# Scan stage of a two-layer decoder: C read through DMA-repeated rows, both readings on GpSimd, operand splits divided over three places

## What is computed

```python
xp = jnp.einsum('bld,ed->ble', x, Wx)          # 64 + 2 * 16 columns
dt_x, B, C = xp[..., :64], xp[..., 64:80], xp[..., 80:96]
dt = softplus(einsum('blr,dr->bld', dt_x, Wdt) + bdt)
dA  = exp(einsum('bld,dn->bldn', dt, A))       # n = 16 states
dBx = einsum('bld,bln,bld->bldn', dt, B, x)
h_t = dA_t * h_{t-1} + dBx_t
y_t = einsum('bdn,bn->bd', h_t, C_t);  y = y + x * D
```

## Time and profile before

| | us |
|---|---|
| median of 3 runs | 1063.38 (1063.21 to 1065.33) |
| profiled execution | 1063.77 |
| its span | 1061.7 |
| busy in the span: PE, DVE, ACT, POOL | 910.1, 805.7, 685.1, 519.6 |
| mean granted TensorE clock | 0.949 of 2.4 GHz |
| scan loop, first product to last reading | 264.7 to 395.9 |
| cross attention, g = 0 to 31 | from about 425 |

### The profile page before, as it was taken

How to read it: one execution, slowest core, us unless ns; L and a number is a source line. 1 busy time by engine, 2 the same in 40 slices (tenths; PEclk the granted TensorE clock), 3 DMA queues, 4 the chain that set the end, 5 groups by cost and what they waited for, 6 DMA issues and landing times.

```text
span 1061.7 us, 16111 instructions
## 1 busy us (share of the span) xinstructions
PE 910.1 (86%) x5404; PEld 578.2 (54%) x5420; DVE 805.7 (76%) x1360; ACT 685.1 (65%) x1601; POOL 519.6 (49%) x407
## 2 busy tenths in 40 slices
PE   5888899565667675799999999999999898999998
PEld 3666544242222222566666777777777565656665
DVE  4578789898999998778888777777877766654554
ACT  2656479787899834788777776887776355532232
POOL 4322346351787832667777666667665443400000
PEclk9899899887798998999999999999999999999999
DMA  9832104000000000000000062111002421222221
GB/s 331 328 137 101 59 18 161 9 1 0 0 1 0 1 0 0 1 1 2 1 1 22 23 174 81 40 41 38 1 1 68 149 64 51 71 66 90 68 65 43
DMA packets 36390, 61.32 MB, mean 58 GB/s; under 512 B 5106, under 2 KB 25010, under 8 KB 34772
## 3 DMA queue, kind: packets, MB, share of 16 engines
q1 hardware_dynamic: 36308, 60.30, 17.3%
HBM read 59.17 MB, written 1.12 MB: 57 GB/s over the span
## 4 chain that ended last, share of the span: by engine, by line
PE 46%; DVE 24%; issue 11%; ACT 11%; POOL 5%; DMA 2%; SPq 0%; DVEq 0%; ACTq 0%; POOLq 0%
PE ps L2414 12%; PE ps L2443 6%; ACT ps L2254 5%; DVE arena L1118 4%; PE ps L1978 3%; DVE ps L1114 3%; PE ps L1991 3%; PE ps L451 2%; PE ps L1970 2%; DVE arena L1123 2%; POOL arena L2335 2%; PE ps L1945 1%; PE ps L491 1%; DMA wide<-in_w_down 1%; PE ps L727 1%
## 5 line engine op out<-in xcount | busy, mean ns | idle before, releaser
L2335 POOL TENSOR_TENSOR arena<-arena 128x4 f32<-128x4 f32 x96 | 98.8, 1029 | 44.6 <-DVE arena L2100 41.9
L2246 ACT ACTIVATE arena<-ps,ones 128x512 f32<-128x512 f32 x96 | 68.2, 786 | 60.5 <-PE ps L1952 60.5
L2461 DVE TENSOR_TENSOR arena<-ps,arena 128x512 f32<-128x512 f32 (+1 forms) x56 | 38.7, 691 | 90.2 <-ACT ps L2454 90.2
L2254 ACT ACTIVATE ps<-ps,arena 128x128 f32<-128x128 f32 x256 | 89.3, 365 | 21.5 <-DVE arena L2079 21.5
L2454 ACT ACTIVATE ps<-ps,arena 128x512 f32<-128x512 f32 (+1 forms) x56 | 36.9, 660 | 87.9 <-PE ps L2414 87.6
L2414 PE MATMUL ps<-XT,wide 128*128 128x512 f16 (+1 forms) x384 | 92.3, 379 | 1.1 <-DVE arena L2480 0.9
L2079 DVE TENSOR_REDUCE arena<-ps 128x4 f32<-128x512 f32 x64 | 43.7, 689 | 53.3 <-PE ps L1962 53.3
L2443 PE MATMUL ps<-wide,arena 128*128 128x256 f16 (+1 forms) x672 | 83.0, 274 | 0.1
L1945 PE MATMUL ps<-wide,arena 128*128 128x512 f16 x256 | 66.8, 396 | 13.7 <-ACT arena L2246 7.1
L2443 PEld LDWEIGHTS ps<-wide,arena 128*128 128x128 f16 (+3 forms) x672 | 65.8, 98 | 20.6 <-issue 1.8
L1118 DVE TENSOR_TENSOR_SCAN arena<-arena,ps 128x1024 f32<-128x1024 f32 x32 | 73.2, 2287 | 1.5 <-POOL arena L1257 0.5
(11 more groups left out here) (343 smaller groups left out, 2426.4 us busy)
## 6 DMA issues: line engine op xcount, KB each, us to landing
arena<-comb_rows SPq DMA_DIRECT2D x26, 256.0 KB, 3.1
side<-in_wproj SPq DMA_DIRECT2D x4, 1024.0 KB, 5.4
arena<-in_w_down SPq DMA_DIRECT2D x7, 512.0 KB, 3.9
wide<-in_w_down SPq DMA_DIRECT2D x1, 3584.0 KB, 16.3
side<-in_w_gate SPq DMA_DIRECT2D x1, 3520.0 KB, 18.8
side<-in_w_up SPq DMA_DIRECT2D x1, 3520.0 KB, 12.0
wide<-in_w_gate SPq DMA_DIRECT2D x2, 1728.0 KB, 12.0
side<-in_w_up SPq DMA_DIRECT2D x3, 1024.0 KB, 9.2
```

The source lines that it names most:

```text
L2246: act.activation(flat(turned[g % 2][:, MAXB * j:MAXB * j + MAXB, :]), ps[:, j, :], ACT.Identity, scale=wt[:, 0:1], bias=wt[:, 1:2]).then_i ...
L2254: last = act.activation(ps[:, 4 + t, i * P:(i + 1) * P], ps[:, 4 + t, i * P:(i + 1) * P], ACT.Exp, bias=mx[:, t, i:i + 1], accum_out=den[: ...
L2335: pool.tensor_tensor(rs[:, j, :], var[:, j, :], minus_half[:, j, :], ALU.pow).then_inc(rs_ready, 1)
```

## The change

B stays as it was: PE spreads its row for each step, now always into banks 2c of PSUM. C is written to DRAM once (`rows_dram`, 16 rows of 1024) from `dt_rows`, into which ACT now copies all 96 rows instead of 64; SP then brings row n back repeated over the 128 partitions, into one of two buffers `c_rows`, once the readings of n - 2 are done. `c_copy`, its ACT copy and C's spreading go. POOL makes both readings. DVE has only products and scans in the loop. ACT and POOL have one split in each n (16 in the loop), five more behind the loop (`TAIL`, buffers unsplit[0] and c_rows[0]; they stand ahead of the cross attention's stream on both engines), and one each in iterations 2, 4, 6, 8 and 10 of the cross attention (`later`, one buffer). The chunks are put into another order, so that the first 21 are what the first iterations need; PE waits for 21 before the first projection and for all 26 in iteration 15. SP's small loads for the cross attention move ahead of the rows.

```diff
...
     dA = [A.take([N]) for _ in range(2)]
-    c_copy = A.take([N])
+    c_rows = [A.take([N])]
     state = [A.take([N]) for _ in range(2)]
...
     unsplit = [A.take([k.proj.SPLIT]), k.XN[:, 0:k.proj.SPLIT // D, :].rearrange("p b d -> p (b d)")]
+    c_rows.append(A.take([N]))
+    assert A.at <= 15080, A.at
+    rows_dram = k.nc.dram_tensor("scan_rows", (NST, N), F32, kind="Internal").ap()
     A = Arena(k.arena, 15080)
...
-    dt_rows = state[1]
+    dt_rows = c_rows[1]
     R0, R1 = DTR, DTR + 2 * NST
...
     b_psum = k.sem("sc_b_psum")
-    c_psum = k.sem("sc_c_psum")
+    c_moved = [k.sem(f"sc_c_moved{i}") for i in range(2)]
     dA_ready = k.sem("sc_dA_ready")
...
     state_ready = k.sem("sc_state_ready")
-    c_taken = k.sem("sc_c_taken")
     read0_ready = k.sem("sc_read0_ready")
...
     def banks(i):
         return ps[:, i:i + 2, :].rearrange("p a b -> p (a b)")
-
-    def home(n, c):
-
-        return 2 * ((n + c) % 2)
...
     def sync(sp):
...
             sp.dma_start(dst, src).then_inc(w_loaded, 16)
+        k.load_cross_small(sp)
+        sp.wait_ge(low_ready, 2)
+        sp.dma_start(rows_dram, dt_rows[R0 + NST:R1, :]).then_inc(c_moved[1], 16)
+        sp.wait_ge(c_moved[1], 16)
+        for n in range(NST):
+            if n == 1:
+                sp.wait_ge(dt_psum, 2)
+                sp.wait_ge(parts_ready, 1)
+            wait(sp, read1_ready, n - 1)
+            sp.dma_start(c_rows[n % 2], rows_dram[n:n + 1, :].broadcast_to([P, N])).then_inc(c_moved[n % 2], 16)
...
     def vector(dve, link):
...
-        dve.wait_ge(low_psum, 2)
-        rows = banks(6)[R0:R1, :]
+        dve.wait_ge(low_ready, 2)
+        rows = dt_rows[R0:R1, :]
         link(dve.tensor_copy(high, rows))
...
         for i, (n, c) in enumerate(STEPS):
-            product = banks(home(n, c))
+            product = banks(2 * c)
             dve.wait_ge(b_psum, i + 1)
...
             dve.tensor_tensor_scan(state[c], dA[c], product, 0.0, ALU.mult, ALU.add).then_inc(state_ready, 1)
-            if c:
-                dve.wait_ge(state_ready, i + 1)
-                dve.wait_ge(c_taken, n + 1)
-                wait(dve, summed, 2 * n - 1)
-                dve.tensor_tensor(read[1], state[1], banks(home(n, 0)), ALU.mult).then_inc(read1_ready, 1)
...
         dve.wait_ge(k.xt_psum, 12)
-        dve.wait_ge(w.split, len(w.chunks))
+        dve.wait_ge(w.split, NST)
         dve.wait_ge(summed, len(STEPS) - 1)
...
             act.wait_ge(low_psum, j + 1)
-            act.copy(dt_rows[0:DTR, 512 * j:512 * j + 512], ps[0:DTR, 6 + j, :]).then_inc(low_ready, 1)
+            act.copy(dt_rows[0:R1, 512 * j:512 * j + 512], ps[0:R1, 6 + j, :]).then_inc(low_ready, 1)
         for c in range(KC):
...
                            scale=decay[:, c, n:n + 1]).then_inc(dA_ready, 1)
-            if i < len(w.chunks):
-                w.split_scalar(act, i, unsplit[i % 2])
-            if c:
-                act.wait_ge(c_psum, n + 1)
-                wait(act, read0_ready, n)
-                act.copy(c_copy, banks(home(n, 0))).then_inc(c_taken, 1)
+            if c == 0:
+                w.split_scalar(act, n, unsplit[n % 2])
+        for i in range(NST, NST + w.TAIL):
+            if i == NST + 1:
+                act.wait_ge(read1_ready, NST - 1)
+            w.split_scalar(act, i, (unsplit[0], c_rows[0])[i % 2])
...
     def tensor(pe):
...
-        def spread(n, first, bank, done):
+        def spread(n, c):
...
             for j in range(2):
-                last = pe.matmul(ps[:, bank + j, :], pick[0:K3, first + n:first + n + 1].broadcast_to([K3, P]), parts[0:K3, 512 * j:512 * j + 512],
+                last = pe.matmul(ps[:, 2 * c + j, :], pick[0:K3, n:n + 1].broadcast_to([K3, P]), parts[0:K3, 512 * j:512 * j + 512],
                                  start=True, stop=True)
-            last.then_inc(done, 1)
+            last.then_inc(b_psum, 1)
...
         def accumulate(i):
...
         pe.wait_ge(parts_ready, 1)
-        spread(0, 0, home(0, 0), b_psum)
+        spread(0, 0)
         pe.wait_ge(dt_relu, 2)
-        spread(0, 0, home(0, 1), b_psum)
+        spread(0, 1)
         for n in range(NST):
-            if n:
-                accumulate(2 * n - 1)
-            pe.wait_ge(state_ready, 2 * n + 1)
-            spread(n, NST, home(n, 0), c_psum)
             if n:
...
             if n + 1 < NST:
+                pe.wait_ge(state_ready, 2 * n + 1)
+                spread(n + 1, 0)
+            if n:
+                accumulate(2 * n - 1)
+            if n + 1 < NST:
                 pe.wait_ge(state_ready, 2 * n + 2)
-                spread(n + 1, 0, home(n + 1, 0), b_psum)
-                pe.wait_ge(read1_ready, n + 1)
-                pe.wait_ge(c_taken, n + 1)
-                spread(n + 1, 0, home(n + 1, 1), b_psum)
+                spread(n + 1, 1)
         accumulate(len(STEPS) - 2)
...
         for i, (n, c) in enumerate(STEPS):
-            if i < len(w.chunks):
-                w.split_pool(pool, i, unsplit[i % 2])
-            if c == 0:
-                pool.wait_ge(c_taken, n + 1)
-                pool.wait_ge(state_ready, i + 1)
-                wait(pool, summed, 2 * n)
-                pool.tensor_tensor(read[0], state[0], c_copy, ALU.mult).then_inc(read0_ready, 1)
+            if c:
+                w.split_pool(pool, n, unsplit[n % 2])
+            else:
+                pool.wait_ge(c_moved[n % 2], 16 * (n // 2 + n % 2 + 1))
+            pool.wait_ge(state_ready, i + 1)
+            wait(pool, summed, i - 1)
+            pool.tensor_tensor(read[c], state[c], c_rows[n % 2], ALU.mult).then_inc((read0_ready, read1_ready)[c], 1)
+        for i in range(NST, NST + w.TAIL):
+            w.split_pool(pool, i, (unsplit[0], c_rows[0])[i % 2])
...
         self.centring += [self.kvx[:, c, 0:G * HD] for c in range(KC)]
-        self.chunks = [(k.wide, self.base[m] + c * self.COLS[m] + n, self.factor[:, c, j:j + 1])
-                       for j, m in enumerate(self.ORDER) for c in range(KC)
-                       for n in range(0, self.COLS[m], self.SPLIT)]
+        def of(*names):
+            return [(k.wide, self.base[m] + c * self.COLS[m] + n, self.factor[:, c, j:j + 1])
+                    for j, m in enumerate(self.ORDER) if m in names for c in range(KC)
+                    for n in range(0, self.COLS[m], self.SPLIT)]
+
+        half = NQ * D
+        self.chunks = of("q", "k", "v")
+        self.chunks += [(k.side, n, self.ranged[:, 6:7]) for n in range(0, half, self.SPLIT)]
+        self.FIRST = len(self.chunks)
+        self.chunks += [(self.ct, n, self.ranged[:, 5:6]) for n in range(0, KC * B * S, self.SPLIT)]
         self.chunks += [(k.wide, n, self.ranged[:, 4:5])
                         for n in range(self.kvx_at, self.kvx_at + KC * 2 * G * HD, self.SPLIT)]
-        self.chunks += [(self.ct, n, self.ranged[:, 5:6]) for n in range(0, KC * B * S, self.SPLIT)]
-        self.chunks += [(k.side, n, self.ranged[:, 6:7]) for n in range(0, 2 * NQ * D, self.SPLIT)]
+        self.chunks += of("qx")
+        self.chunks += [(k.side, half + n, self.ranged[:, 6:7]) for n in range(0, half, self.SPLIT)]
...
     def raw(self, m, c):
...
-    def split_scalar(self, act, i, tmp):
+    TAIL = 5
+
+    def split_scalar(self, act, i, tmp, buffers=2):
         if i == 0:
...
         tensor, at, scale = self.chunks[i]
-        wait(act, self.split, i - 1)
+        wait(act, self.split, i + 1 - buffers)
         act.mul(tmp, tensor[:, at:at + self.SPLIT], scale).then_inc(self.scaled, 1)
...
         self.combT = a.take([4 * S])
+        self.weights_at = a.at
         self.weights = [a.take([4 * S]) for _ in range(3)]
...
     beside = range(19, 19 + moe.EARLY)
+    later = range(2, 2 + 2 * (len(w.chunks) - NST - w.TAIL), 2)
+    unsplit = k.arena[:, moe.weights_at:moe.weights_at + w.SPLIT]
     squaring = (12, 14, 18, 19, 20, 21, 22)
...
     def place(g):
...
-    def sync(sp):
-        sp.wait_ge(k.x_done, 2)
+    def load_small(sp):
         for dst, src in ((norms, a["head_norms"]), (smooth, a["smooth"]),
...
         moe.load_small(sp, w_loaded)
+
+    k.load_cross_small = load_small
+
+    def sync(sp):
         sp.wait_ge(xq_ready, B)
...
         turn_x(0)
-        pe.wait_ge(w.split, len(w.chunks))
+        pe.wait_ge(w.split, NST + w.TAIL)
         for j in range(3):
...
             nxt = g + 1 < NG
+            if g + 1 == 2 * B:
+                pe.wait_ge(w.split, len(w.chunks))
             if nxt:
...
                     take_turned(g + 1, j)
+            if g in later:
+                w.split_scalar(act, NST + w.TAIL + later.index(g), unsplit, 1)
             if g in squaring:
...
                 round_c(g - 1)
+            if g in later:
+                w.split_pool(pool, NST + w.TAIL + later.index(g), unsplit)
             if g % 2 == 0 and 0 < g and (g + 4) // 2 < B:
...
```

## The result

| | before | after |
|---|---|---|
| median | 1063.21 (5 runs, 1061.60 to 1065.33) | 1070.36 (5 runs, 1067.89 to 1072.03) |
| profiled execution, and its span | 1063.77, 1061.7 | 1067.89, 1066.1 |
| busy in the span: PE, DVE, ACT, POOL | 910.1, 805.7, 685.1, 519.6 | 894.8, 778.6, 671.5, 557.9 |

A forecast was written before the change was run, and what follows sets the result against it. VectorE was taken to bound the scan loop (8.16 us per n), a ring of engine waits the cross attention's first half. -13.6 + 9.05 = -4.55 from 1063.77 gave 1059.2, less 0.39 for the median 1058.8; range 1054.5 to 1064.5.

The forecast's parts named there:

- Each split costs 1.81, five of them 9.05 us lost: Cross attention, iterations 2, 4, 6, 8, 10: ScalarE's part delays 1.36 us, GpSimd's late roots a further 0.45.
- pairs of 27.01 for 27.0: Cross attention, g from 2 to 11: two iterations were to take 27.0 us instead of 25.2.
- the square root 14.0 earlier for 13.6: Behind the scan loop: batch 0's square root was to move from 402.69 to 389.1, 13.6 us saved.
- The loop: Scan loop: VectorE stays the bound at 3.46 us per step, 6.92 per n, with GpSimd over 95% busy.
- The rows of C: Scan loop: row DMAs land in 4 to 5 us, below the 6.9 available, so they cost nothing.
- the rival of late rows: Scan loop: rows landing at 8 us lose 7.7 us, giving 1066.5; chance 0.07.
- The end of the loop: Behind the loop: table load stands directly behind the last cast, no longer hidden; square root at 389.1, 13.6 us saved.
- What the five splits give back there was put at 6: Behind the loop: the splits delay the square root from about 383 to 389.1, giving back 6 of some 20 us.
- VectorE held by the splits: Cross attention: each GpSimd split holds a bf16 tensor_scalar 1.64 us, five cost 8.2, giving 1067.0; chance 0.13.
- The loop does not get it: Scan loop: GpSimd's waits raise the period to 7.18 us, 4.2 lost, giving 1063.0, no change; chance 0.08.
- The splits cost less: Cross attention: only ScalarE's part costs, 6.8 us, giving 1056.5, or all hidden, 1049.8; chance 0.12.
- the rival that came nearest: Cross attention: VectorE's bf16 tensor_scalar held by the splits, 8.2 us lost, giving 1067.0; chance 0.13.

The follow-up runs named there:

- Experiment 1: Changed kernel with GpSimd's split behind add_x instead of in front of it in cross-attention iterations 2, 4, 6, 8, 10: 1057.94 us, 0.9925 of before.
- Experiment 6: Changed kernel with all 26 splits in the scan loop, none behind it or in the cross attention: 1064.67 us, 1.0004 of before.
- experiment 10: Experiment 9 with three splits behind the loop, seven late ones in iterations 11 to 17, and add_x(2) at the head of iteration 1: 1042.67 us, 0.9796 of before.
- experiment 2: Changed kernel with ten splits behind the loop (TAIL = 10) and none in the cross attention: 1060.61 us, 0.9963 of before.
- experiment 3: Changed kernel with ScalarE's scale and cast ahead of the three turned tiles and GpSimd's split behind add_x: 1059.90 us, 0.9953 of before.
- experiment 4: Experiment 3, but with GpSimd's split ahead of add_x as in the changed kernel: 1059.71 us, 0.9940 of before.
- experiment 9: Changed kernel, late splits in iterations 11 to 15, cast ahead of turned tiles, GpSimd's part behind round_c, TensorE's wait divided: 1051.34 us, 0.9882 of before.

## Why the prediction was wrong

The forecast of 1058.8 was wrong, and so were its sign and its range. The step that failed is one term of the sum, "Each split costs 1.81, five of them 9.05 us lost". It measured 22.5.

- **Where it failed.** The prediction says "GpSimd: its split starts when the cast has ended ... and frees GpSimd 2.09 later at 521.96. The root of the first heads ... follow". The root follows only if add_x is already done. The diff puts the split in front of add_x, and I had costed GpSimd's queue as if it stood behind: a step of the queue that the split was moved past was left out. GpSimd waits 4.32 us with add_x behind the wait, and the roots come 2.1 us later still. Experiment 1 sets the order that I had costed, and the numbers of the path are then as predicted: pairs of 27.01 for 27.0, 8.8 us for 9.05, the square root 14.0 earlier for 13.6. Shown. That the whole time comes within 1 us of the forecast too (1057.94 for 1058.8) is partly luck: beside experiment 1 the kernel before ran at 1064.45, not 1063.38, and the stretch from iteration 12 on was 1.6 us shorter with no part of the change to explain it.
- **What it cost.** 147.5 - 133.8 = 13.7 us between after and experiment 1 in iterations 2 to 11: 2.07 in each of the first two pairs, and 3.09, 3.17 and 3.31 in the others. Five times 2.07 makes 10.4, and the rest, 3.4, stands in the pairs that begin with iterations 6, 8 and 10. There TensorE's eight matmuls of L2009 took 1.92, 1.89 and 1.37 us instead of 1.04, at the lower clock (last section). The 2.07 is net of whatever the freed L2144 gave back; no run separates the two.
- **The loop.** 3.46 per step was predicted and 3.45 measured; no idle time that counts; the scans unchanged at 2287 ns with GpSimd beside them. GpSimd was busy 104.56 of the 110.40 us from the first product to the end of the last scan, 94.7%, where over 95% was expected. Right but for that 0.3.
- **The rows of C.** 4 to 5 us taken, 3.5 measured, never waited for. Right, and the rival of late rows did not occur.
- **The end of the loop.** The square root was to move by 13.6 and moved by 14.0, with the table load no longer hidden and straight behind the last cast. Right. What the five splits give back there was put at 6. Experiment 6, with none behind the loop, has the square root 8.85 us after the start of the last scan and after has it at 15.85, so it was about 7.0 (an estimate from two kernels); experiments 10 and 2 show that from the fourth on a split costs 2.2.
- **The rivals.** VectorE held by the splits was priced at 1.64 us each with the remark that a shift of 1 us would bring them together. In the kernel after it did not act, as argued: beside the split (481.77 to 483.89) VectorE has a maximum that reads PSUM and then waits for ScalarE, L1866 keeps 0.43 us in the even iterations, and L2144 is even freed there. In experiments 3 and 4 it acted at 1.81 each. "The loop does not get it" would be true with all 26 splits in it (experiment 6), not with 16. "The splits cost less" needed another place (experiment 9).
- **Range and chances.** Had the order been read, the forecast would have put the roots some 2.1 us later (add_x, 2.12) in each pair, 10.6 in all, and come to 1069; the clock's 3.4 would still have been missing. The range did not allow for a misread queue, and its upper end took in only the near part of the rival that came nearest.

## What to carry to other kernels

When a waiting instruction is inserted into an engine's stream, write down what stood behind that place in the old stream and in which idle time it ran: that idle time is what the wait now takes. Work moved to GpSimd cost VectorE nothing here beside its f32 work, and up to 1.8 us beside a 16-bit tensor_scalar from and to SBUF; and that was lost time only where the path runs through this instruction (0.1 us per split in iterations 12 to 15 of experiment 9). So place it by what VectorE does at that moment.
